# 64-byte entries in the experts' lists, and their clear behind the first loads, in a vision block with mixture of experts on one core

## The chip, the cores and the metric

The kernel runs on 1 core of one Trainium2 chip. The metric is the device time of one execution in microseconds, the median of several runs. A core has five engines with an instruction stream each: TensorE (PE; its weight loads are listed as PEld), VectorE (DVE), ScalarE (ACT), GpSimd (POOL) and SyncE (SP). They synchronize by semaphores. DMAs are issued from SP, ACT and POOL and run on 16 DMA engines. The profile is of one execution; "idle before" is the time an engine stood still ahead of an instruction, with what released it.

## The reference, cut to what matters

Images (64 of 224 x 224 x 3) are cut into patches and projected to 197 tokens of 192 features each. An attention block with 12 heads and a causal mask follows, with a residual and a layer norm. Then a mixture of 8 experts, top 2, with a capacity:

```python
N = 64 * 197                      # 12608 tokens
capacity = int(1.2 * N / 8)       # 1891
logits = xf @ Wg
scores, idx = top_k(logits, 2); weights = softmax(scores)
for k in range(2):
    pos = cumsum(onehot(idx[:, k]))                 # rank of a token in its expert's list
    buf[expert, rank] = token                       # entries past the capacity are dropped
    xg = xpad[buf]                                  # gather the tokens of each expert
    h = xg @ W1; act = h[..., :H] * silu(h[..., H:]); ye = act @ W2
    out = out.at[buf].add(w_buf * ye)               # scatter-add, weighted
h = layernorm(h + out)
```

## The kernel before

It has two blocks, one after the other: `attention_block` and `expert_block`. Each writes out the instruction streams of all five engines.

**Attention block.** The 64 images are 32 pairs. `run_bodies` runs a loop over 36 bodies; each body has 12 steps, and in each step the engines work on several pairs at once, at different stages: embedding of pair i+1, queries, keys and values of pair i, scores and values of the pairs before, projection, norm and routing behind. The order of the work in a body is written out by hand (`PIECES`, `EMBED`, the lags `LAG` and `LAG_PV`).

- SP loads the weights (L325 to L331, the last one `tid`) and the first pair's x, then the second pair's x tile by tile (L334), each as soon as GpSimd has split the tile before it (`s_xlo`). In the bodies it stores q and k to DRAM and spreads them back (L341 to L358), and stores the normed tokens (L378).
- ScalarE splits the weights (L460, L462), then x of pair 0 in six tiles (`x_round`, L465). In the bodies it makes exp of the scores (L487, L489), copies and splits, and loads x two pairs ahead (L565).
- GpSimd sets buffers (L401, L404), then masks p (L427, L431), takes the low parts of x (L409), and issues the scatters to the lists (L443).
- VectorE sets q, k and y with memsets (L765 to L770), prepares weights (L772 to L788), and in the bodies takes row maxima (L829, L832), the routing's ranks and slots (L899 to L964), and so on.

**The lists.** For each expert and each of the two choices, the routing keeps a list of SEG = 1920 slots in DRAM, `expert_lists` of shape [NSLOT, ROW], NSLOT = 30720. An entry is a weight (column 0) and a token's row number (column 1, an integer), so ROW = 2 and an entry takes 8 bytes. VectorE writes weight and row number of a pair's tokens into the tile `entry` [128, 4, 2, ROW], one of two, and the slot numbers into `slot`. In stage 5, steps 0, 1, 3, 4, 6, 7, 9 and 10 of a body, GpSimd issues one scatter each (L443): for one of four tiles of tokens (128 or 69 rows) and one of the two choices, one entry a row to the slot that `slot` holds. The first scatter waits for `s_clear`. ScalarE ahead of `pay` and VectorE ahead of `slot` wait for the scatters of two pairs before (`s_sc`), and GpSimd waits for all of them at the end of the block.

Slots that no token takes must hold weight 0 and a row number out of range (`FAR_ROW`). The tile `blank` [128, 240, 2] holds that, set by two memsets of GpSimd, and one DMA from ACT's queue (L457) clears the lists with it: it is ScalarE's first instruction and waits for `s_blank`.

**Expert block.** 80 chunks of 384 slots go through the experts. SP loads the entries of a chunk (L1105) into `e_entry` [128, 3, ROW], one of 8 and four chunks ahead. GpSimd gathers their rows of 1024 bytes (L1142); TensorE turns them (L1225) and does the two layers (L1242; L1255, L1262); VectorE and ScalarE scale by the weight in the entry (L1348, L1289); GpSimd adds the result to the tokens (L1162). A last norm follows.

Of the kernel before, what the change touches and what calls it, by code (L numbers as in the profile page):

```python
# [23 lines left out]
F32 = mybir.dt.float32  # L24
# [9 lines left out]
P = 128  # L34
# [18 lines left out]
TILE3 = 3 * P  # L53
SEG = -(-CAP // TILE3) * TILE3
NSLOT = E * K2 * SEG
ROW = 2
XW = C + C - P
FAR = 1.0e6
FAR_ROW = 1000000
# [141 lines left out]
def attention_block(nc, d):  # L201
    with ExitStack() as ctx:
        def sb(name, shape, dt):
            return ctx.enter_context(nc.sbuf_tensor(name, shape, dt))

        def sem(name):
            return ctx.enter_context(nc.semaphore(name))
# [16 lines left out]
        iota8, kbase = sb("iota8", [P, E], F32), sb("kbase", [P, 4, K2], F32)  # L224
        valid, tid = sb("valid", [P, 4], F32), sb("tid", [P, 4], F32)
        half = sb("half", [P, 4], F32)
        blank = sb("blank", [P, NSLOT // P, ROW], F32)
        word_v, word_p = sb("word_v", [1, NWORDS], F32), sb("word_p", [1, NWORDS], F32)

        x = sb("x", [P, KT, TP], F32)  # L230
# [23 lines left out]
        pay = [sb(f"pay{n}", [P, 4, C], F32) for n in range(2)]  # L254
        entry = [sb(f"entry{n}", [P, 4, K2, ROW], F32) for n in range(2)]
        top = sb("top", [P, 4, E], F32)
# [18 lines left out]
        s_blank, s_clear = sem("blank_ready"), sem("lists_cleared")  # L275
# [48 lines left out]
        def _(sp):  # L324
# [36 lines left out]
            def body(i, turn, par, stages):  # L361
                g = body_at(i)
                for s in range(STEPS):
                    n = (i - 1) * STEPS + s
                    if 1 in stages and s in (2, 3, 5):
                        if s == 2:
                            wait(sp, s_s, (i - 1) * STEPS)
                            sp.wait_ge(s_qset, 5)
                        store_qk(g, par, (2, 3, 5).index(s))
                    if s == 8 and 4 in stages:  # L370
                        p, po_ = i - 3, 1 - par
                        sp.wait_ge(s_x1, p + 1)
                        for t, (im, hf, _, _) in enumerate(TILES):
                            at = bass.ds(p * (2 * T) + (im * T + hf * P), REAL[t])
                            src = pay[po_][0:REAL[t], t, :]
                            for dst, part in ((d["x1"][at, :], src), (d["xin"][at, 0:C], src),
                                              (d["xin"][at, C:XW], src[:, P:C])):
                                sp.dma_start(dst, part).then_inc(s_st1[po_], 16)  # L378
                    if s == 7 and 1 in stages:

                        wait(sp, s_st, (i - 2) * STEPS + 6)
                        sp.wait_ge(s_qset, 5)
                        sp.wait_ge(s_qkw[par], (turn + 1) * (QW * 16))
                        spread_q(par, 0)
                        spread_k(par, 0)
                    if s == 9 and 1 in stages:
                        wait(sp, s_st, (i - 1) * STEPS)
                        spread_q(par, 1)
                    if s == 10 and 1 in stages:
                        spread_k(par, 1)  # L390
# [62 lines left out]

        @block.scalar
        def _(act):
            act.wait_ge(s_blank, 1)
            act.dma_start(d["lists"].rearrange("(p a) c -> p (a c)", p=P),  # L457
                          blank[:].rearrange("p a c -> p (a c)")).then_inc(s_clear, 16)
            act.wait_ge(s_w, 16 * (len(loads) + 3))
            act.activation(wtok_hi[:], wtok, ACT.Copy).then_inc(s_whi, 1)  # L460
            act.wait_ge(s_wg, 2)
# [2 lines left out]
            def x_round(p, t):  # L464
                act.activation(x_hi[:, t], x[:, t], ACT.Copy).then_inc(s_xhi, 1)  # L465

            act.wait_ge(s_x, 16 * KT)
            for t in range(KT):
                x_round(0, t)

            def body(i, turn, par, stages):
                g = body_at(i)
# [97 lines left out]
        def _(pe):  # L570
# [94 lines left out]
            def body(i, turn, par, stages):  # L665
                g = body_at(i)
                for s in range(STEPS):
# [33 lines left out]
                    for name in g.pieces(s):  # L701
# [19 lines left out]
                        elif name[0] == "V":  # L721
                            t, hp = int(name[1]), 1 - par
                            g.wait_free(pe, name)
                            _, _, col, rows = TILES[t]
                            c = slice(col, col + rows)
                            w, v = slice(2 * C, WA), slice(2 * C, 3 * C + E)
# [247 lines left out]
def expert_block(nc, d, out):  # L974
# [15 lines left out]
    with ExitStack() as ctx:  # L990
        def sb(name, shape, dt):
            return ctx.enter_context(nc.sbuf_tensor(name, shape, dt))
# [9 lines left out]
        rows = [sb(f"rows{n}", [P, 3, XW], F32) for n in range(2)]  # L1002
        entry = [sb(f"e_entry{n}", [P, 3, ROW], F32) for n in range(NB)]
        x0_hi = [sb(f"ex0_hi{n}", [P, TILE3], F32R) for n in range(2)]
# [390 lines left out]
def build(nc, d, out):  # L1395
    d = dict(d)
    d["qk"] = nc.dram_tensor("qk_features", [2, 2, 2, 2 * C, TI], F32).ap()
    d["x1"] = nc.dram_tensor("x1_tokens", [N, C], F32).ap()
    d["xin"] = nc.dram_tensor("x1_wide", [N, XW], F32).ap()
    d["lists"] = nc.dram_tensor("expert_lists", [NSLOT, ROW], F32).ap()  # L1400
    attention_block(nc, d)
    expert_block(nc, d, out)
# [83 lines left out]
```

## Time and profile before

| | us |
|---|---|
| median of 3 runs | 2357.99 |
| lowest and highest | 2357.78, 2363.21 |
| the profiled execution's own time | 2355.76 |
| its span, first to last instruction | 2354.0 |
| TensorE matmuls busy in the span | 2140.5 (91%) |
| VectorE, ScalarE, GpSimd busy | 1590.6, 1083.2, 1576.6 |
| mean granted TensorE clock | 0.965 of full |

The profiled execution is one run more, with the profiler on. Its span is 1.8 us shorter than its time. A busy share is an average over both blocks; the scatters lie between 164.1 and 1358.4 us, the loads of entries after that.

### The profile page before, as it was taken

Reading aid. Unit: us, or ns where it says so; the run is one execution under the profiler, and the core shown is the slowest. Engines: PE = TensorE matmul, PEld = TensorE weight load, DVE = VectorE, ACT = ScalarE, POOL = GpSimd, SP = SyncE. Lnnn points to the kernel's source line nnn. Section 1 sums busy time; section 2 is a strip of 40 time slices with the busy share of each in tenths; the row PEclk is TensorE's granted clock in tenths of the full one; section 3 lists DMA queues with packets and bytes.
Section 4 is the critical chain, followed back from the end, with each engine's and each line's share of the span. In section 5 each row is a group of like instructions: output and inputs, shape, how many; then the busy total and the mean of one; then the engine's idle time right before and its main releaser. Section 6 shows DMA issues by size and latency. Waiting matters only on the chain. (4 is left out here: it accounts for less than half of the span.)

```text
span 2354.0 us, 48984 instructions
## 1 busy us (share of the span) xinstructions
PE 2140.5 (91%) x14772; PEld 2070.2 (88%) x14772; DVE 1590.6 (68%) x4287; ACT 1083.2 (46%) x2840; POOL 1576.6 (67%) x2326
## 2 busy tenths in 40 slices
PE   4999999999999999999999559999999999999990
PEld 4899898999989999999988459999999999999980
DVE  4577777877777777777777436666666666666556
ACT  2344444444444444444444225454545454544545
POOL 3356676767666767676765557777777777767666
PEclk9999999999999999999999679999999999999995
DMA  5658888776676565655643133201010101000338
GB/s 155 153 119 123 137 127 142 130 133 137 140 124 139 135 135 136 134 137 133 139 111 84 34 112 62 44 6 26 2 29 3 28 3 26 2 2 15 54 48 332
DMA packets 232530, 219.72 MB, mean 93 GB/s; under 512 B 91027, under 2 KB 212754, under 8 KB 231376
## 3 DMA queue, kind: packets, MB, share of 16 engines
q1 hardware_dynamic: 134800, 146.55, 26.7%
q10 hardware_dynamic: 43328, 56.78, 12.9%
q0 software_dynamic: 54272, 14.76, 5.1%
q8 instruction: 68, 1.11, 0.2%
q14 instruction: 62, 0.51, 0.1%
HBM read 152.91 MB, written 95.25 MB: 105 GB/s over the span
## 5 line engine op out<-in xcount | busy, mean ns | idle before, releaser
L1162 POOL DMA_INDIRECT x_tokens<-yout,e_entry x240 | 382.0, 1592 | 182.1 <-DVE yout L1348 133.5
L651 PE MATMUL Y<-p,vp 128*102 128x198 f32 x1536 | 361.0, 344 | 17.6 <-ACT ysb L482 13.0
L443 POOL DMA_INDIRECT expert_lists<-entry,slot x256 | 288.1, 1126 | 54.1 <-issue 54.1
L1363 DVE TENSOR_TENSOR a<-UP,gate 128x384 f32<-128x384 f32 x320 | 178.6, 558 | 211.7 <-ACT gate L1300 169.8
L487 ACT ACTIVATE p<-ST 128x396 f32<-128x396 f32 x384 | 191.7, 499 | 264.5 <-PE ST L623 247.9
L1255 PE MATMUL Y<-w,a_hi 128*128 128x384 f32 x960 | 304.4, 354 | 2.0 <-DVE a_lo L1353 2.0
L1142 POOL DMA_INDIRECT rows<-x_wide,e_entry x240 | 250.3, 1043 | 77.4 <-issue 72.4
L1300 ACT ACTIVATE gate<-GT 128x384 f32<-128x384 f32 x320 | 157.6, 492 | 290.1 <-PE UP L1242 267.8
L141 POOL TENSOR_TENSOR word_p<-word_p 1x1 f32<-1x1 f32 x416 | 85.8, 206 | 304.6 <-ACT p L489 295.3
L409 POOL TENSOR_TENSOR x_lo<-x,x_hi 128x396 fp32r<-128x396 f32 x192 | 208.2, 1086 | 91.1 <-ACT x_hi L465 89.0
L651 PEld LDWEIGHTS Y<-p,vp 128*102 128x102 f32 x1536 | 221.6, 170 | 32.2 <-issue 11.4
L829 DVE TENSOR_REDUCE rm<-S 128x2 f32<-128x256 f32 x384 | 161.7, 421 | 117.6 <-PE S L642 106.9
L832 DVE TENSOR_REDUCE rm<-S 70x2 f32<-70x396 f32 x384 | 213.9, 557 | 0.0
L629 PE MATMUL S<-k,q 96*128 96x128 f32 x768 | 185.8, 243 | 25.2 <-DVE rm L832 18.6
L1262 PE MATMUL Y<-w,a_lo 128*128 128x192 f32 x960 | 206.8, 256 | 0.0
L655 PE MATMUL Y<-p,vp 70*102 70x70 f32 x1536 | 191.8, 247 | 1.9 <-POOL p L431 1.9
L655 PEld LDWEIGHTS Y<-p,vp 70*102 70x102 f32 x1536 | 185.7, 171 | 3.0 <-POOL p L431 2.6
L629 PEld LDWEIGHTS S<-k,q 96*128 96x128 f32 x768 | 147.4, 192 | 40.4 <-DVE rm L832 28.3
L1255 PEld LDWEIGHTS Y<-w,a_hi 128*128 128x128 f32 x960 | 180.9, 189 | 2.3 <-DVE a_lo L1353 2.2
L849 DVE RECIPROCAL rd<-ysb 6x198 f32<-6x198 f32 x128 | 177.4, 1386 | 4.7 <-ACT ysb L482 0.8
L1348 DVE SCALAR_TENSOR_TENSOR yout<-Y,e_entry,ylo 128x192 f32<-128x192 f32 x240 | 100.3, 418 | 117.0 <-ACT ylo L1289 105.4
L1353 DVE TENSOR_TENSOR a_lo<-a,a_hi 128x384 fp32r<-128x384 f32 x320 | 178.3, 560 | 0.0
(181 smaller groups left out, 6400.1 us busy)
## 6 DMA issues: line engine op xcount, KB each, us to landing
x<-in_xt ACTq DMA_DIRECT2D x180, 198.0 KB
q<-qk_features SPq DMA_DIRECT2D x384, 74.2 KB
k<-qk_features SPq DMA_DIRECT2D x192, 148.5 KB
qk_features<-qk_hi SPq DMA_DIRECT2D x96, 198.0 KB
qk_features<-qk_lo SPq DMA_DIRECT2D x96, 198.0 KB
e_raw<-in_wexp SPq DMA_DIRECT2D x8, 1408.0 KB, 6.7
rb<-rd ACTq DMA_DIRECT2D x128, 74.2 KB
t_x<-x_tokens SPq DMA_DIRECT2D x15, 576.0 KB, 7.5
```

Source lines behind the costliest of these rows:

```text
L409: pool.tensor_tensor(x_lo[:, t], x[:, t], x_hi[:, t].bitcast(F32), ALU.subtract)\
L443: pool.indirect_dma_start(d["lists"][:, :], bass.IndirectOffsetOnAxis(ap=slot[o][0:REAL[t], t, c:c + 1], axis=0), entry[o][0:REAL[t], t, c ...
L487: act.activation(p32[b][:, :, 0:TI], ST[0][:, 0:TP].rearrange("p (h c) -> p h c", h=2), ACT.Exp, scale=SCALE)
L629: pe.matmul(S[0][:, b * P:(b + 1) * P], qt[rows, im, b, j, 0:P], kt[rows, im, j, 0:P], start=(b == 0), stop=False)
L651: return pe.matmul(Y[0:VW1, 0:TI], v0, p32[b][:, hh, 0:TI], start=start, stop=stop)
L655: pe.matmul(Y[0:VW1, P:TI], v1, p32[b][0:T1, hh, TI:TI + T1], start=False, stop=False)
L832: dve.tensor_reduce(rm[im][0:T1, 1, j:j + 7:6], S[1][0:T1, 0:TP].rearrange("p (h c) -> p h c", h=2), AX.X, ALU.max, negate=True).then_inc( ...
L1142: pool.indirect_dma_start(rows[cc % 2][:, t, :], None, d["xin"][:, :], row_of(cc, t), bounds_check=N - 1, oob_is_err=False).then_inc(s_row ...
L1162: pool.indirect_dma_start(d["x1"][:, :], row_of(cc, t), yout[q][:], None, bounds_check=N - 1, oob_is_err=False, compute_op=ALU.add)\
L1255: return pe.matmul(y[:, 0:2 * C], a_hi[q][:, m, c], w2[e][:, m].rearrange("p a b -> p (a b)"), start=(m == 0), stop=(m == HM - 1))
L1262: pe.matmul(y[:, 0:C], a_lo[q][:, m, c], w2[e][:, m, 0], start=False, stop=False)
L1363: dve.tensor_tensor(a32[m % 2][:], UP[m % 2][:, 0:TILE3], gate[m % 2][:], ALU.mult)\
```

## The change

An entry takes ROW = 16 columns, 64 bytes, of which the first two are used as before and the others hold zero. The tiles `entry` and `e_entry` and the DRAM tensor grow with ROW; the scatters and loads move whole entries. `blank` holds only BLANK = 24 entries a partition, and the clear repeats it 10 times over the 240 entries that a partition's share of the lists has: 1280 runs of 24 x 64 = 1536 bytes, where there were 128 runs of 1920. The clear goes from the head of ScalarE's stream to behind the six tiles of x of pair 0.

```diff
-ROW = 2
+ROW, BLANK = 16, 24
...
-        blank = sb("blank", [P, NSLOT // P, ROW], F32)
+        blank = sb("blank", [P, BLANK, ROW], F32)
...
         @block.scalar
         def _(act):
-            act.wait_ge(s_blank, 1)
-            act.dma_start(d["lists"].rearrange("(p a) c -> p (a c)", p=P),
-                          blank[:].rearrange("p a c -> p (a c)")).then_inc(s_clear, 16)
             act.wait_ge(s_w, 16 * (len(loads) + 3))
             act.activation(wtok_hi[:], wtok, ACT.Copy).then_inc(s_whi, 1)
             act.wait_ge(s_wg, 2)
...
             act.wait_ge(s_x, 16 * KT)
             for t in range(KT):
                 x_round(0, t)
+            act.wait_ge(s_blank, 1)
+            act.dma_start(d["lists"].rearrange("(p n a) c -> p n (a c)", p=P, a=BLANK),
+                          blank[:].rearrange("p a c -> p (a c)").unsqueeze(1)
+                          .broadcast_to([P, NSLOT // P // BLANK, BLANK * ROW])).then_inc(s_clear, 16)
```

## Rows read from the trace of the kernel before

**Rows 1.** The page's head: span, busy time, DMA share in 40 slices.

```profile
span 2354.0 us, 48984 instructions
...
PE 2140.5 (91%) x14772; PEld 2070.2 (88%) x14772; DVE 1590.6 (68%) x4287; ACT 1083.2 (46%) x2840; POOL 1576.6 (67%) x2326
...
DMA  5658888776676565655643133201010101000338
```

**Rows 2.** The chain that ended last, by engine.

```profile
PE 38%; POOL 2%; issue 1%; DMA 1%; DVE 0%; ACT 0%; POOLq 0%; SPq 0%; ACTq 0%
```

**Rows 3.** Waits of TensorE, 200 to 1350 us: total, times, longest.

```profile
PE S L629 <- DVE rm L832: 14.7, 30, 2.9
```

**Rows 4.** Tile p, 200 to 1350 us: who waited for it.

```profile
PEld Y L651: 13.3, 26
...
PE Y L651: 3.5, 11
PEld Y L655: 2.6, 2
PE Y L655: 1.9, 2
```

**Rows 5.** Tensor expert_lists: durations in ns, first and last start, landing of the clear.

```profile
L443 POOL DMA_INDIRECT expert_lists<-entry,slot x256: 983/1187/1628, 164.1 to 1358.4; - x128
...
DMA to landing us min/median/max: 6.1/6.1/6.1
```

**Rows 6.** Groups of GpSimd, 200 to 1350 us: busy, mean ns, idle before.

```profile
L443 POOL DMA_INDIRECT expert_lists<-entry,slot x241 | 271.2, 1125 | 50.3 <-issue 50.3
L409 POOL TENSOR_TENSOR x_lo<-x,x_hi 128x396 fp32r<-128x396 f32 x156 | 168.4, 1080 | 33.8 <-ACT x_hi L465 31.9
L427 POOL TENSOR_SCALAR_AFFINE_SELECT p<-p 128x256 f32<-128x256 f32 x345 | 152.2, 441 | 0.0
```

**Rows 7.** Groups of GpSimd in the expert block, 1380 to 2300 us.

```profile
L1142 POOL DMA_INDIRECT rows<-x_wide,e_entry x236 | 246.1, 1043 | 75.5 <-issue 71.6 <-PE XT L1225 3.9
```

**Rows 8.** Timeline of GpSimd: start, duration; a 128-row scatter, then a 69-row one.

```profile
1350.05 0.98 POOL L443 DMA_INDIRECT expert_lists<-entry,slot  x1 [0.30 <-issue]
1351.34 1.18 POOL L443 DMA_INDIRECT expert_lists<-entry,slot  x1 [0.30 <-issue]
```

**Rows 9.** DMA queues, 200 to 1350 us: the scatters' queue (packets, MB, share).

```profile
q0 software_dynamic: 7680, 0.28, 1.1%
```

**Rows 10.** DMA queues, 0 to 16 us: ACT's queue.

```profile
q10 hardware_dynamic: 144, 0.25, 4.0%
```

**Rows 11.** Timeline of the opening, ScalarE and VectorE.

```profile
15.25 1.48 ACT L460 ACTIVATE wtok_hi<-vp 128x1536 fp32r<-128x1536 f32 x1 [9.73 <-DMA tid<-in_tid]
...
15.91 0.44 DVE L770 MEMSET y<- 1x198 f32 x2
16.38 0.57 DVE L772 TENSOR_TENSOR addend<-postab,biastab 128x396 f32<-128x396 f32 x1
...
17.55 1.50 ACT L462 ACTIVATE wa_hi<-vp 128x1552 fp32r<-128x1552 f32 x1 [0.81 <-DVE wg_centred L778]
```

**Rows 12.** Timeline of ScalarE, 18 to 37 us.

```profile
18.95 2.64 ACT L465 ACTIVATE x_hi<-x 128x396 fp32r<-128x396 f32 x6
31.41 0.54 ACT L505 ACTIVATE h_hi<-ht 128x396 fp32r<-128x396 f32 x1 [9.83 <-DVE ht L804]
...
36.02 0.52 ACT L465 ACTIVATE x_hi<-x 128x396 fp32r<-128x396 f32 x1
```

**Rows 13.** DMA queues, 20 to 36 us: SP's queue, the six tiles of x.

```profile
q1 hardware_dynamic: 864, 1.22, 28.5%
```

**Rows 14.** The chain of work, 1364 to 1368 us: start, duration.

```profile
1364.40 1.70 DMA e_entry<-expert_lists
```

**Rows 15.** Busy time by window: five engines, granted clock, DMA share, GB/s.

```profile
31.00:36.00 5.00, 3.51 (x18) 3.18 (x18) 1.40 (x3) 0.95 (x2) 0.00 (x0) 1.00 0.00 0
40.00:60.00 20.00, 9.92 (x48) 8.08 (x47) 3.34 (x7) 4.37 (x9) 5.72 (x6) 0.84 0.88 197
```

## Prediction

> **What bounds the kernel now.** I read the page's head first: TensorE is busy for 91% of a span of 2354.0 us [rows 1]. The chain that ended last runs through TensorE, with small shares for GpSimd, DMA and issue [rows 2]. The kernel has two stages. Pairs of images pass through embedding and attention until about 1360 us, and there the DMA engines are mostly 50 to 80% busy [rows 1]. The experts follow, with the DMA engines at 0 to 20%. The changed bytes belong to the first stage when they are written (256 scatters) and to the second when they are read (80 loads). So I asked of each: who waits for it?
>
> In a full stretch of attention (200 to 1350 us) TensorE's largest wait is for VectorE's row maxima, 14.7 us in all [rows 3]. No row of TensorE there names the lists. GpSimd issues the scatters, and its other work for TensorE is masking p. For the masked p, matmuls and weight loads together wait 13.3 + 3.5 + 2.6 + 1.9 = 21.3 us in those 1150 us [rows 4]. That is the only door by which a scatter could reach TensorE. The first scatter starts at 164.1 us and the last at 1358.4 us [rows 5].
>
> **Part 1: the scatters carry 64 bytes a row in place of 8.** There are still 256 instructions, each with one descriptor for a row, 128 or 69 of them. On GpSimd a scatter took 1125 ns in the mean [rows 6]. Does it depend on bytes? The gather of the expert stage moves 128 rows of 1024 bytes, 128 times the bytes of an entry, in 1043 ns [rows 7]. A scatter of 128 rows of 8 bytes took 0.98 us and one of 69 rows 1.18 us [rows 8]. So the duration follows neither the bytes nor the count of rows upward. I cost the change on GpSimd at 0. Bounds: every scatter like the shortest form, (1.125 - 0.98) x 256 = 37 us less of GpSimd; or, by the spread of the two forms the other way, (1.18 - 1.125) x 256 = 14 us more. TensorE sees of this at most what it waits for p: from -21 us to about 14 x 21.3/1150 = +0.3 us, unless the masks become late in their own right.
>
> On the DMA engines the scatters' queue holds 1.1% of 16 engines between 200 and 1350 us [rows 9]. Even at twice that, the engines stay under 80% there. The landings are awaited two bodies later (8 scatters a body and 241 in 1150 us make 38 us a body, so 76 us), by ScalarE ahead of pay and by VectorE ahead of slot, and by GpSimd at the end of the stage. I take 0, with 0 to -1 us at the end of the stage, where the last landing is on the path.
>
> The chip may write 64 bytes more cheaply than 8, but 1.1% of the engines' time is all that could be saved, and no wait hangs on it. The Trainium skill, "DMA: Bandwidth & Descriptors", Specifications, speaks against a gain: under 512 bytes the engine reads, modifies and writes. By that rule both 8 and 64 bytes pay it, and the change saves nothing; by the opposite reading it saves part of the 1.1%. The sum is the same by either, and no row here tells the two apart.
>
> **Part 2: the clear moves and grows.** The lists have 30720 entries: 245,760 bytes before, 1,966,080 after, eight times as many, in 1280 descriptors of 1536 bytes in place of 128 of 1920.
>
> *Removed from the opening.* The old clear (240 KB) is the only large user of ACT's queue in the first 16 us: 4.0% of 16 engines x 16 us, so 0.64 us of all engines [rows 10]. So the last small load (tid), for which ScalarE starts at 15.25 us, may land up to 0.64 us earlier. Nothing follows from it: VectorE sets its start-up tiles with memsets until 16.35 us, reaches addend at 16.38 us, and ScalarE's second split (17.55 us) waits for VectorE's wg_centred [rows 11]. ScalarE's first split and TensorE's average would start earlier into a wait that ends at the same time. I take 0; bounds 0 and -0.6 us. The memsets of blank and entry on GpSimd (480 elements become 384, twice 64 bytes become 512) change by tenths of a microsecond, in the first 4 us; GpSimd's next work, the split of x, waits for ScalarE's x_hi, which starts at 18.95 us [rows 12].
>
> *Added behind the first splits.* ScalarE finishes x_hi of pair 0 at 18.95 + 2.64 = 21.6 us and then issues the clear. Its next instruction starts at 31.41 us [rows 12], so even an issue of some microseconds is covered. On the queue, the clear meets the six tiles of x for pair 1, which SP issues from 23.48 us. Price of the clear: by bytes 8 x 0.64 = 5.1 us of all engines; by descriptors 10.24 engine-us / 128 = 80 ns, x 1280 / 16 = 6.4 us. I take 6.4. The six tiles of x cost 28.5% of 16 us = 4.6 us [rows 13]. Both together are 11 us. Counted from 23.5 us (21.6 us and what a small load needs to land, 1.70 us [rows 14]) they are done by 34.5 us even if x comes last in the line. In the run before, the tiles are in by 31 us, and the DMA engines then stand at 0.00 until 36 us [rows 15]. ScalarE first needs them at 36.02 us [rows 12]. So 1.5 us of slack is left at worst: 0 us on the path. GpSimd's wait for the clear comes at the first scatter, 164.1 us, more than 120 us later.
>
> The bound from above: the old clear needed 6.1 us from issue to landing [rows 5]. Were that its rate and not queueing, the new one would take 8 x 6.1 = 49 us and reach into the first spreads of q and k (40 us on).
>
> The Trainium skill, "DMA: Bandwidth & Descriptors", Rules for kernel authors, warns that a leading zero-stride dimension of c copies confines a DMA to c engines. Here the 10 copies stand behind the 128 partitions; were it confined to 10 all the same, the clear would take 6.4 x 1.6 = 10.2 us on these, x would be in at 38.3 us, 2.3 us late, and the time would be 2360.3. I give that 0.02, inside the case of no change below; no run so far shows it.
>
> **Part 3: the reads.** 80 loads of 128 rows of 24 bytes become 192 bytes a row: 24 KB each, about 2 MB over 900 us in which the DMA engines are nearly idle. Only the first is on the path, 1.70 us [rows 14]. The same 128 descriptors, still short: 0, bounds 0 and +0.2 us. The scalars on ScalarE and VectorE and the indices on GpSimd read one element a row as before, at another stride: 0.
>
> **The sum.** 0 (scatters) + 0 (opening) + 0 (clear) + 0 (reads). The profiled execution took 2355.76 us for a span of 2354.0; the median of the three runs shown is 2357.99, 2.2 us above it. Against the median: 2358.0 us. The small bounds alone give -1.6 to +0.5 us; the three runs spread by 5.4 us. What a measurement of this kernel can tell from no change is about 0.3%, 7.1 us.
>
> **The rivals.**
>
> *Faster: short writes hold GpSimd.* If a scatter of 8 bytes a row costs GpSimd time that one of 64 does not, masks come sooner. For it: steps 0, 1, 3 and 4 of a body put a mask, a scatter and a split of x on GpSimd: 0.44 us for the mask's larger half, 1.13 and 1.08 us, with gaps nearly all of a step of 1150/345 = 3.3 us [rows 6]. Against: the 1024-byte gather's 1043 ns beside the 0.98 us of the 128-row scatter. Price: all of the wait for p, 21.3 us, gives 2337; half of it gives 2347. It decides from a mean of L443 under about 1.0 us. Chance 0.07.
>
> *Slower: the clear is in the way.* If it runs at the rate of its old landing, it is still running from 40 to 60 us, when the spreads of q and k of pairs 0 and 1 have their turn and TensorE waits for them. At equal shares the engines' work there, 20 us at 0.88 [rows 15], takes up to twice as long: up to +17.6 us, 2376 us; the middle is 2367. For it: ten times the descriptors, and the landing of 6.1 us. Against: that landing was among loads that filled the engines, and the packets themselves took 0.64 us of them. It decides when the clear costs more than 7.9 us of all engines (36.0 - 23.5 - 4.6), and passes 0.3% only when the delay exceeds 7 us. Chance 0.06.
>
> *Nothing moves.* Writes, clear and reads are all hidden, as the sum has it: 2358, own range 2353 to 2363. Chance 0.87. This is also the case in which whole 64-byte entries save the DMA engines something that no engine waits for.
>
> **How the numbers follow.** The likeliest case gives 2358.0. The range, 2350 to 2365, takes its spread, the small bounds, and the near part of either rival; the far parts, 2337 to 2350 and 2365 to 2376, hold under 0.1. Faster by over 0.3%: 0.07; slower: 0.06; within: 0.87.
>
> **What the profile would show.** Right: L443 still at 1.0 to 1.2 us; the clear issued near 21.6 us with its packets gone by about 30 us; ScalarE's x_hi of pair 1 still near 36.0 us, behind h and not behind x; its 15.25 us start perhaps 14.6 with 17.55 unchanged; the first e_entry still at 1.7 us; first scatter near 164 us, stage end near 1360 us. Wrong: a mean of L443 that moved by over 0.1 us with TensorE's wait for p; a wait of ScalarE for x near 36 us; TensorE waiting for q or k before 100 us; or a stage end moved by several microseconds with no row to account for it, which would mean a coupling of writes and spreads that I did not see.

## The result, and the profile after

The changed kernel takes 2343.71 us in the median of 5 runs (2337.33 to 2344.79), where the kernel before takes 2357.99 on the same chip (5 runs, to 2365.08). The ratio is 0.992, with an interval of 0.9902 to 0.9939: faster, by 14 to 23 us. That is outside the range of the prediction, which said 2358.0 with 2350 to 2365 and gave "faster by over 0.3%" a chance of 0.07. Beside other runs on two more chips the same kernel gave 0.9963 (0.9946 to 0.9980) and 0.9959 (0.9938 to 0.9979), since the kernel before stands there at 2347 to 2348 us. So the sign is firm, and its size is nearer 0.4% than 0.8%. The experiments below are compared with the kernel before on their own chip.

The page of the changed kernel: span, busy time, DMA share in 40 slices, and the rate of bytes under it.

```profile
span 2342.8 us, 48984 instructions
...
PE 2140.4 (91%) x14772; PEld 2073.5 (89%) x14772; DVE 1581.8 (68%) x4287; ACT 1079.3 (46%) x2840; POOL 1579.4 (67%) x2326
...
DMA  6656565656565656565643134201010101000338
GB/s 185 148 123 144 132 145 131 143 130 143 130 142 130 142 131 142 129 144 128 145 94 79 32 119 64 44 8 28 4 31 5 30 5 28 4 3 17 56 48 334
```

TensorE does the same work in 11.2 us less. The DMA row is what differs: it swings between 5 and 6 through all of attention, where [rows 1] had 8 and 7 in the first third and fell to 5 and 6 later. The row of bytes ahead of the change was no higher there. The same bytes took the DMA engines longer, and not in the scatters' own queue. From 200 to 1350 us SP's queue (q1) and ACT's (q10) hold 41.7% and 20.8% of the 16 engines before, and 37.2% and 17.3% after, for nearly the same packets (columns: packets, MB, share; before, then after):

```profile
q1 hardware_dynamic: 101745, 104.44, 41.7%
q10 hardware_dynamic: 34902, 39.87, 20.8%
```

```profile
q1 hardware_dynamic: 101254, 103.83, 37.2%
q10 hardware_dynamic: 34902, 39.87, 17.3%
q0 software_dynamic: 7936, 0.69, 1.4%
```

Two stretches show when, before and then after (columns: PE, PEld, DVE, ACT, POOL busy, granted clock, DMA share, GB/s):

```profile
200.00:400.00 200.00, 190.29 (x1409) 179.92 (x1408) 148.39 (x452) 91.62 (x267) 134.07 (x262) 0.99 0.85 133
800.00:1000.00 200.00, 194.84 (x1465) 185.68 (x1463) 152.33 (x463) 96.10 (x280) 139.13 (x274) 1.00 0.59 133
```

```profile
200.00:400.00 200.00, 195.28 (x1472) 186.67 (x1471) 153.22 (x462) 94.55 (x277) 138.72 (x272) 1.00 0.60 137
800.00:1000.00 200.00, 195.79 (x1474) 187.11 (x1473) 152.35 (x463) 95.01 (x278) 140.75 (x275) 1.00 0.61 137
```

At 133 GB/s in both of its stretches, the kernel before has its DMA engines at 0.85 in one and at 0.59 in the other. In the first one TensorE does 1409 matmuls, in the second 1465. After the change there is no such difference.

The waits of the kernel before in one place of that stretch (TensorE at 372.56 us, VectorE from 355 to 375 us) tell one way in which it reaches TensorE: the spread of nm into q and of the reciprocals rd into rb come late. The changed kernel has no DMA in its waits of 355 to 375 us. From 200 to 1300 us TensorE's matmuls wait 3.0 us for q in three places before, and no such wait is listed after.

```profile
372.56 0.45 PE L617 MATMUL ST<-q,k 97*128 97x396 f32 x1 [2.36 <-DMA q<-nm]
```

```profile
DVE y L840 <- DMA rb<-rd: 2.9, 1, 2.9
```

The other way is longer than these waits and carries no DMA's name. VectorE's y, which reads rb and ysb, takes 0.35 us, but now and then over 1.2 us. It then ends 0.22 or 0.23 us after GpSimd's split of x (x_lo, L409) ends, in all 39 cases of the 17 traces: the instruction is not slow, it waits for GpSimd while its time runs. One case of the kernel before (start, duration):

```profile
695.94 1.04 POOL L409 TENSOR_TENSOR x_lo<-x,x_hi 128x396 fp32r<-128x396 f32 x1
696.68 2.26 DVE L840 TENSOR_TENSOR y<-ysb,rb 96x198 f32<-96x198 f32 x1 [0.60 <-DMA rb<-rd]
697.71 1.01 POOL L409 TENSOR_TENSOR x_lo<-x,x_hi 128x396 fp32r<-128x396 f32 x1
```

y ends at 698.94 us, the second split at 698.72. Behind it the row maxima come late, and TensorE waits 2.9 us for them, the longest wait of [rows 3]. Every trace has one such y between 205 and 215 us. From there to 1150 us the kernel before has four more (249, 410, 685 and 697 us), the changed kernel none. A y can also overlap a split without this: at 219.63 us in the changed kernel it takes 0.35 us beside one. What decides it stays open, and that late spreads move y onto the splits is argued from these counts, not shown one by one.

The lists' rows after, which answer [rows 5]: the scatters span 1179.2 us in place of 1194.3 us, and from the first load of entries to the end it is 992.2 us in place of 989.6. All of the gain is in attention.

```profile
L443 POOL DMA_INDIRECT expert_lists<-entry,slot x256: 982/1186/1762, 165.4 to 1344.6; - x128
L1106 SPq DMA_DIRECT2D e_entry<-expert_lists x80: 319/320/592, 1350.6 to 2203.6; - x80
L468 ACTq DMA_DIRECT2D expert_lists<-blank x1: 647/647/647, 17.6 to 17.6; - x1
```

ScalarE's start of each body (the split of h_hi, one a body) divides the difference. From the starts in the two traces, the intervals in us:

```
before 16.7 38.4 37.3 38.9 39.0 41.2 42.2 39.1 38.9 41.9 39.4 39.2 39.3 39.4 39.0 39.2 39.0 42.8 38.9 39.2 38.9 39.2 38.9 39.1 39.0 39.2 38.9 39.1 39.0 41.8 38.1
after  16.2 40.7 37.3 38.6 38.7 39.2 39.3 39.0 38.8 39.0 38.8 39.0 38.8 39.0 38.8 39.0 38.8 39.0 38.8 39.0 38.8 39.0 38.8 39.0 38.8 39.0 38.8 39.0 38.8 41.7 40.8
```

There are two kinds of loss before. Four bodies (the 6th, 7th, 10th and 18th) are 2 to 4 us too long, 11.6 us together; the 10th has the waits at 372 us, the 7th one of the long y, the 18th two of them. And every body is some 0.15 us longer: 38.9 and 39.2 in turn against 38.8 and 39.0. The second is quiet and goes on where the DMA share is 0.6. So there were two questions: what held up the DMAs, and what made the steady period.

One number from outside the traces helps with the first: with these inputs, the reference's routing sends nearly all tokens to two of the eight experts. Counted from its indices, 7899 of the 25216 entries get a place, and 7726 of these come from the first 16 of 32 pairs: all of them up to pair 5, a third in pairs 8 to 13, one in a hundred after pair 16. The first scatter is at 164 us and a body takes 39, so pair 14 comes at about 710 us: the DMA share falls just as entries stop landing. And since two lists take nearly all, a scatter's entries are neighbours: the 1576 entries of the first two pairs, counted scatter by scatter, lie in 231 pieces of 64 bytes.

### The profile page after: what moved, and what is told of

It is laid out like the page before. It is cut to its first block and busy times, and to the rows that moved or that the text cites. A ratio compares the mean times of both kernels' runs of the same rounds, so it can differ in the third digit from the quotient of the medians.

```text
span 2342.8 us, 48984 instructions
## 1 busy us (share of the span) xinstructions
PE 2140.4 (91%) x14772; PEld 2073.5 (89%) x14772; DVE 1581.8 (68%) x4287; ACT 1079.3 (46%) x2840; POOL 1579.4 (67%) x2326
## 5 line engine op out<-in xcount | busy, mean ns | idle before, releaser
L443 POOL DMA_INDIRECT expert_lists<-entry,slot x256 | 288.5, 1127 | 54.3 <-issue 54.3
L409 POOL TENSOR_TENSOR x_lo<-x,x_hi 128x396 fp32r<-128x396 f32 x192 | 208.4, 1087 | 93.4 <-ACT x_hi L462 91.7
L1263 PEld LDWEIGHTS Y<-w,a_lo 128*128 128x128 f32 x960 | 178.2, 189 | 0.0
```

Source lines behind the costliest of these rows:

```text
L409: pool.tensor_tensor(x_lo[:, t], x[:, t], x_hi[:, t].bitcast(F32), ALU.subtract)\
L443: pool.indirect_dma_start(d["lists"][:, :], bass.IndirectOffsetOnAxis(ap=slot[o][0:REAL[t], t, c:c + 1], axis=0), entry[o][0:REAL[t], t, c ...
L1263: pe.matmul(y[:, 0:C], a_lo[q][:, m, c], w2[e][:, m, 0], start=False, stop=False)
```

## Experiments

### Which part of the change helps

The change has two edits: the entries and the clear. Each was undone alone; two more kernels write 8 bytes an entry but take away the shared 64 bytes, or the landing. The first and the third are edits of the changed kernel, the second and the fourth of the kernel before; that matters for the times, as the last experiment shows, so the DMA share is the plainer sign here.

**The clear at the head again, with 64-byte entries.**

```diff
+            act.wait_ge(s_blank, 1)
+            act.dma_start(d["lists"].rearrange("(p n a) c -> p n (a c)", p=P, a=BLANK),
...
             act.wait_ge(s_w, 16 * (len(loads) + 3))
```

> 64-byte entries as in the change, but the clear stands at the head of ScalarE's stream again (the repeated tile, 1280 runs of 1536 bytes). In the changed kernel the DMA engines' share between 200 and 400 us fell from 0.84 to 0.60 at the same rate of bytes. Theory A (short writes: an 8-byte write to the lists in DRAM holds up other packets at the memory, a 64-byte one does not): about 2344 us, last scatter near 1345 us; the clear among the first loads may cost up to 5 us at the start, since it takes that much of all DMA engines while the loads run, so 2344 to 2349. Rival B (the moved clear is what helped): back to 2358. Rival C (neighbours: eight writes into one 64-byte line collide) and rival D (another place in DRAM, since the tensor is 8 times as large) say the same as A here.

Measured: 2345.37 us, 0.9984 of the kernel before (0.9962 to 1.0006), which is not clear of no change. The DMA share from 200 to 400 us is 0.59, so the stalls stay away without the move. But the clear of 2 MB among the first loads costs:

```profile
19.43 1.49 ACT L461 ACTIVATE wtok_hi<-vp 128x1536 fp32r<-128x1536 f32 x1 [13.71 <-DMA tid<-in_tid]
20.82 1.48 ACT L463 ACTIVATE wa_hi<-vp 128x1552 fp32r<-128x1552 f32 x1
22.21 2.63 ACT L466 ACTIVATE x_hi<-x 128x396 fp32r<-128x396 f32 x6
34.26 0.54 ACT L506 ACTIVATE h_hi<-ht 128x396 fp32r<-128x396 f32 x1 [9.41 <-DVE ht L805]
```

The last small load, tid, releases ScalarE at 19.43 us in place of 15.25 [rows 11], and the first h_hi starts at 34.26 us where the changed kernel has 31.16: 3.1 us, inside the expected 0 to 5. So the move is not what gains over the kernel before; it is what keeps the larger clear from costing 3 us. This trace also has one body of 44.2 us, with a long y at 181 us. It waits for GpSimd's split like that at 696 us in the kernel before, and ends at 183.99 us, the split at 183.77:

```profile
181.08 2.91 DVE L841 TENSOR_TENSOR y<-ysb,rb 96x198 f32<-96x198 f32 x1
182.76 1.01 POOL L409 TENSOR_TENSOR x_lo<-x,x_hi 128x396 fp32r<-128x396 f32 x1
```

It is the only one before 1150 us, beyond the common one, in the twelve traces in which no dense 8-byte entries land; why it comes there stays open.

**8-byte entries, the clear late.**

```diff
-            act.wait_ge(s_blank, 1)
-            act.dma_start(d["lists"].rearrange("(p a) c -> p (a c)", p=P),
...
             for t in range(KT):
                 x_round(0, t)
+            act.wait_ge(s_blank, 1)
+            act.dma_start(d["lists"].rearrange("(p a) c -> p (a c)", p=P),
```

> 8-byte entries as before, but the clear (the whole tile, 128 runs of 1920 bytes) stands behind the six tiles of x. Theory A, and rivals C and D: 2358 us, DMA share 0.8 and more between 200 and 400 us, as before. Rival B (the clear's place): 2344.

Measured: 2346.64 us, 0.9995 (0.9979 to 1.0011): no change. The DMA share from 200 to 400 us is 0.79. The clear's place is not the cause of the gain.

**8 bytes written, at a pitch of 64.**

```diff
-        entry = [sb(f"entry{n}", [P, 4, K2, ROW], F32) for n in range(2)]
+        entry = [sb(f"entry{n}", [P, 4, K2, 2], F32) for n in range(2)]
...
-                            d["lists"][:, :],
+                            d["lists"].rearrange("n (m c) -> (n m) c", c=2),
...
-ch.mark(dve.tensor_tensor(slot[o][:], sl[:], over[:], ALU.add))
+ch.mark(dve.scalar_tensor_tensor(out=slot[o][:], in0=sl[:], scalar=float(ROW // 2), in1=over[:],
+                                 op0=ALU.mult, op1=ALU.add))
```

> As the changed kernel, but only the first 8 bytes of a 64-byte slot are written by the scatters (the slot number is multiplied by 8 by the same instruction that adds the overflow); the clear, the size of the tensor and the loads are those of the change. Theory A (short writes cost by themselves): 2358 us, last scatter near 1358 us, DMA share over 0.8 between 200 and 400 us. Rival C (neighbours in one line collide): 2344, since no two entries share 64 bytes any more. Rival D (size and place of the tensor): 2344.

Measured: 2341.14 us, 0.9964 (0.9943 to 0.9985), DMA share 0.59. Theory A as I had it, that a short write costs by itself, falls here; rival C, that neighbours in the same 64 bytes collide, stands, and so does D (size and place of the tensor), so far.

```profile
200.00:400.00 200.00, 195.06 (x1470) 186.06 (x1469) 152.79 (x462) 95.27 (x279) 139.05 (x271) 1.00 0.59 134
```

**8-byte entries, none lands.**

```diff
-ch.mark(dve.tensor_scalar(over[:], rank[:], float(CAP), FAR,
+ch.mark(dve.tensor_scalar(over[:], rank[:], -1.0e3, FAR,
```

> The kernel before, but every slot number is out of range: all 256 scatters are issued, and no entry is written. The experts then find empty lists, so their part of the output is missing. Theory A and rival C: the stall is gone, 2344 us or a little less, last scatter near 1344 us, DMA share 0.6 between 200 and 400 us. Rival D (place of the tensor) and any theory in which the instructions on GpSimd matter: 2358, last scatter near 1358 us.

Measured: 2340.07 us, 0.9969 (0.9948 to 0.9990), DMA share 0.59, last scatter at 1344.4 us. The 256 instructions are issued as before, so they are not the cause: it takes entries that land. D is weakened and not out, since nothing is written to the small tensor here. The runs below close it: dense 8-byte entries stall in another tensor of 1.2 MB too, and 32-byte ones do not in lists of 1.0 MB.

### The dose

If the stalls come with landing entries, they must last as long as entries land. Three kernels store all 25216 entries in a tensor with room for everyone; they differ in what an entry is. The 8-byte dense one is an edit of the kernel before, the others of the changed kernel, so the place of the tiles (last experiment) differs as well. The experts' lists stay empty in all three, so the experts' part of the output is missing. From here on, theory A in the expectations is that of the neighbours.

```diff
-                            d["lists"][:, :],
+                            d["scratch"][:, :],
...
-ch.mark(dve.tensor_scalar(over[:], rank[:], float(CAP), FAR,
+ch.mark(dve.tensor_scalar(over[:], rank[:], FAR, FAR,
...
+    d["scratch"] = nc.dram_tensor("scratch", [5 * NSLOT, ROW], F32).ap()
```

> The kernel before with 8-byte entries, all 25216 of them stored densely in a separate tensor with room for everyone (no capacity), in place of the 7899 that find a place in the lists (7726 of them from the first 16 pairs); the lists stay empty, so the experts' part of the output is missing. Theory A (neighbours: several engines write 8 bytes each into the same 64 bytes, and other packets wait meanwhile): the DMA share stays above 0.75 in every stretch from 200 to 1200 us, and waits for rb and nm come in all of them; the dense 8-byte kernel lost about 10 us for 7726 entries, so about 2340 + 10 x 25216/7726 = 2373 us. Rival (the stall belongs to the beginning of the kernel and fades by itself): share 0.6 after 700 us as before, time as before.

> The same with whole 64-byte entries, all 25216 stored. Theory A: DMA share 0.6 throughout, 2340 us, as with none landing. If landing entries cost by their number, whatever their size: as the 8-byte twin, about 2373.

> The same with 8 bytes written at a pitch of 64, all 25216 stored. Theory A: 0.6 and 2340, since no two entries share 64 bytes. If a short write costs by itself, only less: a share above 0.65 and a time between the twins.

Measured on one chip:

| all 25216 entries land | us | ratio to before (interval) | DMA share 200 to 400, 800 to 1000 us |
|---|---|---|---|
| 8 bytes, dense | 2357.66 | 1.0048 (1.0030 to 1.0067) | 0.78, 0.76 |
| 64 bytes, dense | 2337.36 | 0.9955 (0.9941 to 0.9969) | 0.59, 0.60 |
| 8 bytes at a pitch of 64 | 2335.70 | 0.9962 (0.9947 to 0.9977) | 0.58, 0.60 |

The 8-byte dense kernel, from 800 to 1000 us, where the kernel before had 0.59:

```profile
800.00:1000.00 200.00, 194.57 (x1460) 185.11 (x1459) 155.01 (x460) 95.18 (x278) 139.63 (x273) 1.00 0.76 137
```

and the only wait of TensorE's matmuls for a DMA in it, 200 to 1300 us:

```profile
PE ST L617 <- DMA q<-nm: 5.8, 4, 2.5
```

The stall no longer fades: it is not the beginning of the kernel. Eight long y (from 365 to 998 us) come with it, where the kernel before has four; the body of 45.3 us holds two of them. The 8-byte dense kernel takes 20 us more than the 64-byte one, less than my 33, and part of the 20 is the place of the tiles. The fairer comparison is with the kernel in which no entry lands, at the same place: 1.0048 beside 0.9969, or 0.8%, some 18 us, across two chips. My price per entry was too high: the loss that it was read from held other things, the place of the tiles among them. Entries that share no 64 bytes cost nothing that shows, 8 bytes long or 64. What costs is writes close together. That they share a piece, and do not merely fall into a small stretch of memory, no run separates: a pitch of 64 bytes spreads a scatter over eight times the range as well.

### How many bytes must be an entry's own

> All 25216 entries stored, densely, 16 bytes each, written whole: four entries share 64 bytes. All landing gave 1.0048 of the kernel before with 8 bytes and 0.9955 with 64. Theory A (neighbours in 64 bytes): between the twins, a DMA share over 0.65, 0.998 to 1.003. If the unit that must be written whole is 32 bytes, two still share it and the stall stays.

> The same with 32 bytes: two entries share 64 bytes, none share 32. Theory A with a unit of 64 bytes: some stall left, DMA share 0.62 to 0.70, 0.997 to 1.001. With a unit of 32 bytes: share 0.60 and 0.9955, as with 64 bytes.

The edit of both is `ROW, BLANK = 4, 24` and `8, 24` in the 64-byte kernel of the dose. Measured: 16 bytes 2342.26 us, 0.9981 (0.9967 to 0.9995), DMA share 0.62; 32 bytes 2337.34 us, 0.9946 (0.9925 to 0.9967), share 0.61, and 0.60 to 0.61 up to 1000 us. Two 32-byte entries share 64 bytes and do not stall, so 64 bytes are not needed, as theory A had it; 32 are enough.

Whether 16 bytes would be enough too, these two do not tell. In the 16-byte kernel `blank` has 384 bytes, and its bodies take 38.9 and 39.2 us in turn, where the 32-byte one has 38.8 and 39.0. By the last experiment that is a matter of the tiles' place, and is worth 0.1 to 0.3% of the 0.35% between the two ratios. Beside the two kernels with the same period and no stall, none landing (0.9969) and the change with its tiles put back (0.9973), 0.9981 is inside the intervals. No body of the 16-byte kernel is too long. What is left is its DMA share: 0.60 to 0.64 in the five stretches of 200 us from 200 to 1200 us, where those two have 0.57 to 0.61.

The real kernel with 32-byte entries:

```diff
-ROW, BLANK = 16, 24
+ROW, BLANK = 8, 24
```

> The changed kernel with 32-byte entries (ROW 8): half the bytes for the clear and the loads, 1280 runs of 768 bytes. If 32 bytes are enough: as the change, 0.996 of the kernel before. If pairs in 64 bytes still collide: 0.998.

Measured: 2336.95 us, 0.9957 (0.9939 to 0.9975), scatters from 163.5 to 1341.1 us. It is as fast as the change on the other chips (0.9963, 0.9959), with half the memory; no run has the two side by side, and their intervals overlap.

### The steady part: the place of the tiles

The period of 38.9 and 39.2 us is there in the kernel with no landing entry too, and that of 38.8 and 39.0 in the one with 8 bytes at a pitch of 64. So the period does not go with the stalls. What goes with it is how large `blank` is, which stands ahead of most tiles in SBUF: 1920 bytes before, 1536 after.

```diff
-        blank = sb("blank", [P, NSLOT // P, ROW], F32)
+        blank = sb("blank", [P, 24, ROW], F32)
+        pad = sb("pad", [P, 336], F32)
```

> The kernel before, 8-byte entries, with the tile blank shrunk to 192 bytes a partition and a pad behind it, so that the tiles after it stand 384 bytes lower in SBUF, as in the changed kernel; the clear repeats the small tile at its old place (1280 runs of 192 bytes). In the quiet part (850 to 1150 us) a body takes 38.9 and 39.2 us in turn in the kernels with 8-byte tiles and 38.8 and 39.0 in those with the change's tiles, landing or not: 0.15 us x 28 = 4 us. If the place of the tiles does it: 38.8 and 39.0 here, and about 0.998 of the kernel before, with the stalls of the short writes still there. If not: 38.9 and 39.2, and 1.000.

Measured: 2340.54 us, 0.9970 (0.9955 to 0.9985), bodies of 38.8 and 39.0 us, with the DMA share still at 0.72 from 200 to 400 us. To close it, each part once alone:

```diff
         blank = sb("blank", [P, BLANK, ROW], F32)
+        pad = sb("pad", [P, 96], F32)      # in the changed kernel
...
         blank = sb("blank", [P, NSLOT // P, ROW], F32)
+        pad = sb("pad", [P, 32], F32)      # in the kernel before
```

> The changed kernel with a pad of 384 bytes a partition behind blank, so that the tiles from word_v to the second pay stand where they stood in the kernel before. Theory (place of the tiles): bodies of 38.9 and 39.2 us in turn, TensorE waits over 2 us for ysb between 850 and 1150 us, and about 4 us more than the changed kernel: 0.998 of the kernel before, with no short-write stalls (DMA share 0.6 from 200 to 600 us). Rival (the period goes with the size of the entries): 38.8 and 39.0, and 0.996.

> The kernel before with nothing changed but a pad of 128 bytes a partition behind blank. With the repeated small tile and 384 bytes lower it gave 0.9970, with bodies of 38.8 and 39.0 us. A shift by 128 bytes up is the same place modulo 512. Theory (place of the tiles): 38.8 and 39.0, 0.997 to 0.998, and the short-write stalls of 200 to 600 us still there (share over 0.7). Rival (the small tile and its many short runs did it): 38.9 and 39.2, and 1.000.

> The changed kernel on the same chip as the two with pads. From the parts: 4 us for the place of the tiles and 4 to 6 us for the stalls of the dense 8-byte entries, 0.996 of the kernel before; 0.002 below the changed kernel with its tiles put back.

> The changed kernel once more, beside the others on one chip. On the chip of the three runs before, 8 bytes at a pitch of 64 gave 0.9964 of the kernel before and none landing 0.9969. Theory A: the change gives the same, 0.996 to 0.997, and what is beyond it in the first comparison (0.992) is the spread of single executions of the kernel before, which is large. If the whole write or the clear's place adds something of its own: 0.992 here too.

Measured, the first three on one chip, the last on another:

| | us | ratio to before (interval) | bodies | DMA share 200 to 400 us |
|---|---|---|---|---|
| change, tiles put back | 2342.04 | 0.9973 (0.9959 to 0.9988) | 38.9, 39.2 | 0.59 |
| before, pad only | 2342.21 | 0.9971 (0.9954 to 0.9988) | 38.8, 39.0 | 0.75 |
| change | 2339.33 | 0.9959 (0.9938 to 0.9979) | 38.8, 39.0 | 0.59 |
| change, once more | 2338.49 | 0.9963 (0.9946 to 0.9980) | 38.8, 39.0 | 0.60 |

ScalarE's h_hi in the quiet part, in the change with tiles put back, and in the kernel before with the pad (start, duration):

```profile
864.66 0.53 ACT L507 ACTIVATE h_hi<-ht 128x396 fp32r<-128x396 f32 x1 [0.45 <-issue]
903.55 0.53 ACT L507 ACTIVATE h_hi<-ht 128x396 fp32r<-128x396 f32 x1 [0.33 <-issue]
942.73 0.53 ACT L507 ACTIVATE h_hi<-ht 128x396 fp32r<-128x396 f32 x1 [0.44 <-issue]
```

```profile
867.87 0.53 ACT L506 ACTIVATE h_hi<-ht 128x396 fp32r<-128x396 f32 x1 [0.44 <-issue]
906.69 0.53 ACT L506 ACTIVATE h_hi<-ht 128x396 fp32r<-128x396 f32 x1 [0.33 <-issue]
945.73 0.53 ACT L506 ACTIVATE h_hi<-ht 128x396 fp32r<-128x396 f32 x1 [0.45 <-issue]
```

38.89 and 39.18 us with the tiles at the old place, 38.82 and 39.04 with 128 bytes of padding in an otherwise untouched kernel. The two parts are thus apart. Each alone gains over the kernel before: the entries 0.27%, the place of the tiles 0.29%. The change, which has both, gains 0.41% on the same chip, with an interval up to 0.62%, and 0.37% on the other, up to 0.54%: that the two add up to 0.56% is not shown. Taken out of the change, the place is worth 2342.04 - 2339.33 = 2.7 us, though the intervals of these two overlap. Where the period comes from can be followed one step. From 850 to 1150 us, TensorE's waits in the kernel before, then in the change:

```profile
PE Y L651 <- ACT ysb L482: 2.8, 12, 0.3
PE S L629 <- DVE rm L832: 2.7, 8, 0.3
PE Y L651 <- POOL p L431: 1.0, 3, 0.3
```

```profile
PE S L630 <- DVE rm L833: 2.4, 7, 0.3
PE Y L652 <- POOL p L431: 1.7, 6, 0.3
PE ST L618 <- ACT p L490: 0.6, 4, 0.2
```

The wait for ScalarE's copy ysb goes. It is 1.8 to 3.0 us in the six kernels with the long period (before, clear late, none lands, 8 bytes all landing, 16 bytes, tiles put back), and at most 1.0 in the eleven with the short one. The shifts that leave the long period are 0 and 1536 bytes down; 384 and 1152 down and 128 up give the short one. That fits a rule modulo 512, or modulo 256, from five places; which tile it is, and why, was not tried.

## Why the prediction was wrong, point by point

**The step that failed** is in part 1: "1.1% of the engines' time is all that could be saved, and no wait hangs on it". I priced the short writes by the time of their own packets. What they cost was the time of others' packets: at 133 to 137 GB/s the engines were at 0.85 in place of 0.60, and SP's and ACT's queues held 62.5% of them between 200 and 1350 us in place of 54.5%. The scatters' own share after is 1.4%, higher than [rows 9], while the engines as a whole are freer. "No wait hangs on it" failed with it: TensorE waited 3.0 us for q, VectorE for rb, and y for GpSimd. The evidence was in my own [rows 1]: a DMA share that falls through attention, at a rate of bytes that does not. I read it as "mostly 50 to 80%", though four slices stand at 80 to 90%, and did not ask why equal bodies load the engines unequally. The last sign of being wrong in the prediction is the one that came: the last scatter at 1344.6 us in place of 1358.4, from a coupling of writes and spreads and, for some 4 us, from the place of the tiles. The case with the chance of 0.87 had room for a saving of the DMA engines, but one that no engine waits for.

**The instruction on GpSimd** was right: L443 lasted 1126 ns in the mean against 1125.

```profile
L443 POOL DMA_INDIRECT expert_lists<-entry,slot x248 | 279.3, 1126 | 52.6 <-issue 52.6
```

TensorE's wait for the masked p went from 21.3 to 21.7 us. So the one faster rival, on GpSimd, was wrong too: its door stayed shut, and that 2343.71 lies between its 2337 and its 2347 is chance. The other door, the DMAs that SP and ScalarE issue for q, k, nm and rb, I never costed. The waits for them are small in total, but a body with one is 2 to 3 us too long, and a y that runs into GpSimd's split waits up to 2.3 us more.

**The Trainium skill's rule** was weighed to no use. The Trainium skill, "DMA: Bandwidth & Descriptors", Specifications, has writes under 512 bytes read, modified and written. By it all sizes here pay, and I took that for "saves nothing". The traces show a large difference in the DMA share at 8 bytes dense (0.72 to 0.78), a small one at 16 (0.60 to 0.64), and none at 32 bytes or for 8 bytes at a pitch of 64 (0.57 to 0.61). The rule does not contradict this, but it says nothing of it.

**The opening** was right to a tenth. ScalarE's first split starts at 14.58 us (predicted 14.6), and the second, behind VectorE, at 17.54 (predicted unchanged).

```profile
14.58 1.48 ACT L457 ACTIVATE wtok_hi<-vp 128x1536 fp32r<-128x1536 f32 x1 [12.49 <-DMA tid<-in_tid]
17.54 1.50 ACT L459 ACTIVATE wa_hi<-vp 128x1552 fp32r<-128x1552 f32 x1 [1.47 <-DVE wg_centred L779]
17.56 0.65 ACTq L468 DMA_DIRECT2D expert_lists<-blank  x1
18.94 2.64 ACT L462 ACTIVATE x_hi<-x 128x396 fp32r<-128x396 f32 x6
...
35.78 0.52 ACT L462 ACTIVATE x_hi<-x 128x396 fp32r<-128x396 f32 x1
```

**The clear**: issued at 17.56 us, not at 21.6. Here ScalarE issued it, though it stands behind the splits of x in the program, before the first of these started at 18.94 us; I had it wait for them. Its queue holds 27.3% of the 20 us from 16 to 36 us, 5.5 us of all engines, between my 5.1 (by bytes) and 6.4 (by descriptors, which I took), and most of it is over before x of pair 1 begins at 23.5. x_hi of pair 1 starts at 35.78 us, behind h: the slower rival did not come about. The Trainium skill's rule on the count of engines ("DMA: Bandwidth & Descriptors", Rules for kernel authors) did not apply, as expected: in the 40 slices from 16 to 36 us the DMA share stands at 90% and more while the clear runs, and ten engines would give 63% at most.

```profile
DMA  0000029999999999477788767878600000000000
...
q10 hardware_dynamic: 1296, 1.97, 27.3%
q1 hardware_dynamic: 864, 1.22, 23.2%
```

What I did not see is what the larger clear would have cost at its old place, 3.1 us; the move is worth that.

**The reads**: the first load of entries took 1.68 us against 1.70 [rows 14]. Right.

**The tiles**: I costed the smaller `blank` at tenths of a microsecond of memset. That it moves the tiles behind it had no term in the sum at all. It was worth 0.15 us a body, some 4 us by the period; by the times 2.7 us within the change, and 0.29% (0.12 to 0.46) alone in the kernel before.

## What to carry to other kernels

When equal work loads the DMA engines unequally at the same rate of bytes, look for something small that is holding them. Here it was scattered writes of 8 bytes close together; 32 bytes an entry, or a pitch of 64, cured it. Price a small write not by its own packet but by what other packets do while it lands. An instruction that is long now and then may be waiting for another engine: compare its end with theirs. And treat a change in the size of any tile as a change in the place of all tiles behind it: pad back to the old place before crediting a fraction of a percent to the edit.

## What the runs showed of the hardware that was not expected

- Dense 8-byte scattered writes to DRAM, all 25216 landing, raise the busy share of the DMA engines from 0.59 to 0.78 at a nearly unchanged rate of bytes (134 and 136 GB/s) and cost some 18 us, against none landing; 16-byte ones raise it to 0.62 and cost no time that shows; 32 and 64 bytes, or 8 bytes at a pitch of 64, nothing. By what mechanism neighbours hold up other queues' packets, the runs don't tell.
- VectorE's y (two inputs in SBUF) and GpSimd's split of x (two inputs too) can hold each other up: in 39 cases y took 1.28 to 2.91 us in place of 0.35 and ended 0.22 or 0.23 us after the split.
- A shift of the tiles in SBUF by 128 bytes a partition, with nothing else changed, gives 0.9971 (0.9954 to 0.9988), and bodies of 38.8 and 39.0 us in place of 38.9 and 39.2.
- A DMA of 1280 runs of 1536 bytes from a repeated tile took 5.5 us of all engines for 1.97 MB, and ScalarE 0.65 us to issue.
- The kernel before has medians of 2358 us (5 runs) beside the first measurement of the change and 2345 to 2348 (21 to 31 runs) on four chips later.
